# Batch 0 of attention: q cuts written and gathered before k, own turned rows for odd batches, first scores between two quarters of the next q and k

## What is computed

```python
qkv = hidden_states @ w_attn + b_attn
q, k, v = jnp.split(qkv, 3, axis=-1)             # 32 heads of 16 columns each
scores = jnp.einsum('bqhd,bkhd->bhqk', q, k) * SCALE
scores = jnp.where(causal[None, None], scores + bias[None], -jnp.inf)
attn = jax.nn.softmax(scores, axis=-1)
out = jnp.einsum('bhqk,bkhd->bqhd', attn, v).reshape(B, S, HIDDEN)
x = x + (out @ w_proj + b_proj)
```

## Time and profile before

| | |
|---|---|
| median of 3 runs | 704.13 us (703.55 to 704.23) |
| the profiled execution | 705.04 us |
| its span in the profile | 703.3 us |
| PE busy | 656.4 us, 93% |
| DVE busy | 478.5 us, 68% |
| ACT busy | 342.0 us, 49% |
| POOL busy | 92.0 us, 13% |
| mean granted clock of PE | 0.988 |

### The profile page before, as it was taken

One profiled execution on the slowest core, in us unless ns is written; L12 is line 12 of the kernel. 1 busy time (PEld: TensorE's weight loads), 2 busy tenths in 40 slices (PEclk: granted clock), 3 DMA queues, 4 the chain that ended last, 5 costly groups with the idle time before them and its releaser, 6 DMA issues.

```text
span 703.3 us, 10157 instructions
## 1 busy us (share of the span) xinstructions
PE 656.4 (93%) x3784; PEld 485.3 (69%) x3784; DVE 478.5 (68%) x906; ACT 342.0 (49%) x534; POOL 92.0 (13%) x189
## 2 busy tenths in 40 slices
PE   5988999999999886999999999999999999999997
PEld 4866688678676664887786665756756555787876
DVE  6755584894788779787693656365364797868565
ACT  5214554524534671442378996476482924435221
POOL 4411002102101042100141010100100220100000
PEclk9989999999999997999999999999999999999999
DMA  8494503505636040000062000000001305000000
GB/s 272 118 266 145 169 14 94 154 27 150 206 98 228 2 160 1 0 1 1 15 229 79 0 1 0 1 0 1 1 0 57 123 0 180 2 30 16 16 31 30
DMA packets 31763, 51.35 MB, mean 73 GB/s; under 512 B 3433, under 2 KB 17132, under 8 KB 30159
## 3 DMA queue, kind: packets, MB, share of 16 engines
q1 hardware_dynamic: 31138, 49.05, 21.8%
q10 hardware_dynamic: 576, 1.64, 1.0%
HBM read 42.09 MB, written 8.40 MB: 72 GB/s over the span
## 4 chain that ended last, share of the span: by engine, by line
PE 77%; DVE 13%; ACT 4%; issue 2%; DMA 1%; ACTq 1%; POOL 1%; SPq 0%; DVEq 0%; POOLq 0%
PE ps L1853 13%; PE ps L1820 12%; PE ps L2041 11%; PE ps L1980 10%; PE ps L1984 5%; PE ps L1683 5%; DVE nmax L1077 3%; PE ps L1761 2%; PE ps L1699 2%; PE ps L1829 2%; PE ps L1663 2%; PE ps L1751 2%; DVE prodT L1590 1%; DVE nmax L1074 1%; ACT sign_junk L966 1%
## 5 line engine op out<-in xcount | busy, mean ns | idle before, releaser
L2041 PE MATMUL ps<-wdT,prodT 128*128 128x512 f32 (+1 forms) x176 | 77.7, 597 | 0.4
L2041 PEld LDWEIGHTS ps<-wdT,prodT 128*128 128x128 f32 (+1 forms) x176 | 32.8, 190 | 40.7 <-issue 38.2
L800 ACT ACTIVATE probsT<-ps 128x1536 f32<-128x1536 f32 x32 | 46.1, 1450 | 28.9 <-PE ps L1751 28.7
L840 ACT ACTIVATE funs<-ps 128x512 f32<-128x512 f32 x16 | 9.5, 596 | 99.0 <-PE ps L1822 88.0
L669 POOL TENSOR_SCALAR ln_spread<-ln_moments 128x1 f32<-128x1 f32 x24 | 6.9, 287 | 299.4 <-DVE ln_moments L1148 299.4
L1154 DVE SCALAR_TENSOR_TENSOR junk<-x_sb,gate_row 128x512 f32<-128x512 f32 x48 | 43.1, 897 | 1.0
L1590 DVE COPY prodT<-ps 128x512 f32<-128x512 f32 (+1 forms) x24 | 13.7, 599 | 40.3 <-PE ps L2030 40.0
L1077 DVE TENSOR_REDUCE nmax<-ps 128x4 f32<-128x1024 f32 x32 | 38.9, 1215 | 0.0
L1417 DVE SCALAR_TENSOR_TENSOR x_sb<-b_row,coef,x_sb 128x512 f32<-128x512 f32 x48 | 37.0, 771 | 1.8
L966 ACT ACTIVATE sign_junk<-mlp_size_next,minus_guess 128x1376 bf16<-128x1376 f32 x24 | 34.6, 1443 | 0.8
L966 ACT ACTIVATE sign_junk<-mlp_size_main,minus_guess 128x1376 bf16<-128x1376 f32 x24 | 34.6, 1442 | 0.7
(11 more groups left out here) (282 smaller groups left out, 1725.0 us busy)
## 6 DMA issues: line engine op xcount, KB each, us to landing
cuts<-parts SPq DMA_DIRECT2D x16, 384.0 KB, 2.8
qst<-cuts SPq DMA_DIRECT2D x48, 128.0 KB, 2.6
w_first_raw<-in_L_ffn_w SPq DMA_DIRECT2D x6, 1024.0 KB, 7.7
w_second_raw<-in_L_ffn_w SPq DMA_DIRECT2D x6, 1024.0 KB, 9.0
kst<-cuts SPq DMA_DIRECT2D x36, 128.0 KB, 2.7
wqkv_raw<-in_L_attn_a_w_attn SPq DMA_DIRECT2D x3, 1024.0 KB, 8.2
wdT<-in_L_attn_b_w_down SPq DMA_DIRECT2D x1, 2560.0 KB, 10.1
wg_raw<-in_L_attn_b_w_gate SPq DMA_DIRECT2D x1, 2048.0 KB, 7.9
```

Source lines behind the costliest of these rows:

```text
L800: nc.scalar.activation(probsT[:, g % 2, :].rearrange("p (k n) -> p k n", k=3), slot[g % 2], ACT.Exp).then_inc(exp_ok.sem, 1)
L2041: last = nc.tensor.matmul(ps[:, Y_BANK, :], prodT[0:m, c, :], wdT[0:m, c, :], start=(c == 0), stop=(c == IC - 1))
```

## The change

The parts of it, with the diff below cut to its core:

1. SP writes q of half 0 as soon as its third part is there, ahead of the six small bias loads, then q of half 1, then gathers q of both halves, each after its own write. ACT writes k of both halves after its last `second_part`, then gathers k of half 0. SP gathers k of half 1 after q.
2. POOL does the cut of batch 0's first quarter ahead of `ln(1)`.
3. Odd batches have turned rows of their own (`odd_rowsT_hi`, `odd_rowsT_lo`), and batch 1 turns into PSUM banks 0 and 1. PE turns the rows of batch 1 in front of the values of batch 0; DVE copies them before the last quarter's rest and makes the low part between the two values.
4. PE makes quarter 0 of batch 1 after the values, and quarter 1 between score groups 1 and 2 of batch 0. DVE makes the rest of quarter 0 after the maxima of group 1 and that of quarter 1 after the maxima of group 3.

```diff
+        odd_rowsT_hi = sb("odd_rowsT_hi", [P, KC, S], F32R)
+        odd_rowsT_lo = sb("odd_rowsT_lo", [P, KC, S], F32R)
...
+        def write_side(eng, b, half, side):
+            need(eng, part3, b, place(b, 2 * half + side) + 1)
+            eng.dma_start(cuts[side, half].rearrange("m (g p) t -> p (m g) t", p=P),
+                          parts[:, side, half].rearrange("p m g t -> p (m g) t")).then_inc(cuts_out[half].sem, 16)
...
         def row_banks(b):
-            return first_rows if b == 0 else work
+            return first_rows if b <= 1 else work
...
+            write_side(sp, 0, 0, 0)
             sp.wait_ge(bias_out, 16)
             sp.wait_ge(bias_zero, 2)
...
-            write_cuts(0, 0)
-            write_cuts(0, 1)
-            gather(0, 0, (0,))
-            gather(0, 1, (0,))
+            write_side(sp, 0, 1, 0)
+            for half in range(2):
+                need(sp, cuts_out[half], 0, 16)
+                send_rows(sp, 0, half, 0)
+            need(sp, cuts_out[1], 0, 16 * 2)
+            send_rows(sp, 0, 1, 1)
...
             constants()
+            cut(0, (0,))
             ln(1)
-            cut(0)
+            cut(0, (1, 2, 3))
...
             second_part(0, 3)
+            for half in range(2):
+                need(act, cuts_out[half], 0, 16)
+                write_side(act, 0, half, 1)
             need(act, cuts_out[0], 0, 16 * 2)
             send_rows(act, 0, 0, 1)
-            need(act, cuts_out[1], 0, 16 * 2)
-            send_rows(act, 0, 1, 1)
...
             residue(0, 1)
+            for j in range(TB):
+                turned_rows_high(1, j)
             residue(0, 3)
             dve.wait_ge(bias_v_in, 16)
-            for j in range(TB):
-                value(0, j)
-            for j in range(TB):
-                turned_rows_high(1, j)
+            value(0, 0)
             for j in range(TB):
                 turned_rows_low(1, j)
-            residue(1, 0)
-            residue(1, 1)
+            value(0, 1)
...
+            def first(g):
+                if g == 1:
+                    residue(1, 0)
+                elif g == 3:
+                    residue(1, 1)
...
-                maxima(b, lambda g: steady(b, g) if b >= 1 else None)
+                maxima(b, first if b == 0 else lambda g: steady(b, g))
...
+            turn_rows(1)
             for j in range(TB):
                 value(0, j)
-            turn_rows(1)
-            for f in range(2):
-                turned_part(1, f)
+            turned_part(1, 0)
             pe.wait_ge(alibi_in, 32)
             pe.wait_ge(consts, 11)
             for g in range(NG):
+                if g == 2:
+                    turned_part(1, 1)
                 scores(0, g)
             turned_part(1, 2)
             maxima(0)
```

More of the change, by code:

```diff
@@ L281, in build @@
         wqkv_lo = sb("wqkv_lo", [P, 3, KC, D], F32R, wqkv_at)
-        qk_bias = sb("qk_bias", [P, 2, HT], F32)
-        at[0] = wqkv_at + 3 * 4 * KC * D + 4 * TB * 2 * D
+        odd_rowsT_hi = sb("odd_rowsT_hi", [P, KC, S], F32R)
+        odd_rowsT_lo = sb("odd_rowsT_lo", [P, KC, S], F32R)
         parts = sb("parts", [P, 2, 2, 3, HT // 2, S], BF16)
@@ L290, in build @@
         wproj_hi = sb("wproj_hi", [P, KC, D], F32R)
-        rowsT_hi = sb("rowsT_hi", [P, KC, S], F32R)
-        rowsT_lo = sb("rowsT_lo", [P, KC, S], F32R)
+        even_rowsT_hi = sb("even_rowsT_hi", [P, KC, S], F32R)
+        even_rowsT_lo = sb("even_rowsT_lo", [P, KC, S], F32R)
         qst = sb("qst", [P, H, S], BF16)
@@ L301, in build @@
         rden = sb("rden", [P, 2, TB * G], F32)
+        qk_bias = sb("qk_bias", [P, 2, HT], F32)
         maskS = sb("maskS", [P, P], BF16)
@@ L488, in place @@
             return turned_order(b).index(f)
+        rowsT_hi, rowsT_lo = (even_rowsT_hi, odd_rowsT_hi), (even_rowsT_lo, odd_rowsT_lo)
         def turn_bank(b, f):
             return ps[:, 2 + f, :] if b == 0 else work[f % 2]
+        def write_side(eng, b, half, side):
+            need(eng, part3, b, place(b, 2 * half + side) + 1)
+            eng.dma_start(cuts[side, half].rearrange("m (g p) t -> p (m g) t", p=P),
+                          parts[:, side, half].rearrange("p m g t -> p (m g) t")).then_inc(cuts_out[half].sem, 16)
         def send_rows(eng, b, half, side):
@@ L533, in _ @@
             sp.dma_start(bias_cuts.rearrange("i (p n) -> p i n", p=P), bias_parts[:, :, :]).then_inc(bias_out, 16)
[L534 to L539, removed]
             def write_cuts(b, half):
@@ L543, in write_cuts, with gather @@
                 for side in range(2):
[L544 to L549, removed]
+                    write_side(sp, b, half, side)
+            def gather(b, half):
                 need(sp, sT_ps, b - 1, (half + 1) * GHALF)
                 need(sp, cuts_out[half], b, 16 * 2)
-                for side in sides:
+                for side in range(2):
                     send_rows(sp, b, half, side)
@@ L567, in load_wide @@
                 sp.dma_start(end[:, :, :], w[:, :, IM:I]).then_inc(here, 16)
-            write_cuts(0, 0)
-            write_cuts(0, 1)
-            gather(0, 0, (0,))
-            gather(0, 1, (0,))
+            write_side(sp, 0, 0, 0)
+            sp.wait_ge(bias_out, 16)
+            sp.wait_ge(bias_zero, 2)
+            for i in range(3):
+                sp.dma_start(bias_proj[32 * i:32 * i + 1, :], bias_cuts[i:i + 1, 0:D]).then_inc(bias_rows, 16)
+                sp.dma_start(bias1[32 * i:32 * i + 1, :, :].rearrange("a e n -> a (e n)"),
+                             bias_cuts[i:i + 1, D:]).then_inc(bias_rows, 16)
+            write_side(sp, 0, 1, 0)
[4 more added lines that the diff above has]
+            send_rows(sp, 0, 1, 1)
             sp.dma_start(x_sb[:, 2 * TB:T, :], x_v[:, 2 * TB:T, :]).then_inc(x_rest, 16)
@@ L655, in ln, with cut @@
                 nc.gpsimd.tensor_tensor(rstd[:, :], spread[:, :], neg_half[:, :], ALU.pow).then_inc(rstd_ok.sem, 1)
-            def cut(b):
-                for k, f in enumerate(turned_order(b)):
+            def cut(b, steps=range(4)):
+                for k in steps:
+                    f = turned_order(b)[k]
                     side, pair = f % 2, f // 2
@@ L744, in turned_rows @@
                     need(act, hT_ps, b, j + 1)
-                    nc.scalar.copy(rowsT_hi[:, :, j * P:(j + 1) * P],
+                    nc.scalar.copy(rowsT_hi[b % 2][:, :, j * P:(j + 1) * P],
                                    row_banks(b)[j].rearrange("p (c t) -> p c t", c=KC)).then_inc(hT_ok.sem, 1)
@@ L1024, in turned_rows_high @@
                 need(dve, hT_ps, b, j + 1)
-                nc.vector.tensor_copy(rowsT_hi[:, :, j * P:(j + 1) * P],
+                nc.vector.tensor_copy(rowsT_hi[b % 2][:, :, j * P:(j + 1) * P],
                                       row_banks(b)[j].rearrange("p (c t) -> p c t", c=KC)).then_inc(hT_ok.sem, 1)
@@ L1030, in turned_rows_low @@
                 at_j = slice(j * P, (j + 1) * P)
-                nc.vector.tensor_tensor(rowsT_lo[:, :, at_j], row_banks(b)[j].rearrange("p (c t) -> p c t", c=KC),
-                                        rowsT_hi[:, :, at_j].bitcast(F32), ALU.subtract).then_inc(hT_low.sem, 1)
+                nc.vector.tensor_tensor(rowsT_lo[b % 2][:, :, at_j], row_banks(b)[j].rearrange("p (c t) -> p c t", c=KC),
+                                        rowsT_hi[b % 2][:, :, at_j].bitcast(F32), ALU.subtract).then_inc(hT_low.sem, 1)
             def turned_heads_low(b, j):
@@ L1639, in turn_rows @@
                 for j in range(TB):
-                    if b >= 1:
+                    if b == 1:
+                        need(pe, hT_low, 0, j + 1)
+                    elif b >= 2:
                         need(pe, v_out, b - 1, j + 1)
@@ L1662, in value @@
                     for c in range(KC):
-                        last = nc.tensor.matmul(work[j], rows[:, c, at_j], weight[:, 2, c, :],
+                        last = nc.tensor.matmul(work[j], rows[b % 2][:, c, at_j], weight[:, 2, c, :],
                                                 start=(i == 0 and c == 0), stop=(i == 2 and c == KC - 1))
@@ L1671, in turned_part @@
                     need(pe, res1, b, f - 1)
-                elif b >= 1:
+                elif b == 1:
+                    need(pe, v_out, 0, f + 1)
+                elif b >= 2:
                     need(pe, hT_low, b, f + 1)
@@ L1683, in turned_part @@
                             last = nc.tensor.matmul(turn_bank(b, f)[:, m * S:(m + 1) * S], weight[:, side, c, columns],
-                                                    rows[:, c, :], start=(i == 0 and c == 0),
+                                                    rows[b % 2][:, c, :], start=(i == 0 and c == 0),
                                                     stop=(i == 2 and c == KC - 1))
```

## The result

The kernel with the change took 709.74 us, the median of 6 runs (706.84 to 710.36), beside 704.44 for the kernel before in 6 runs: a ratio of 1.0062, with a 95% interval of 1.0043 to 1.0082. A second set of 6 runs beside 16 of before gave 707.92 and 703.9, ratio 1.0061 (1.0039 to 1.0083). The change makes the kernel slower by 0.6%, some 4.3 us. The ratio is not the quotient of the two medians, which lie 5.3 us apart in the first set and 4.0 in the second. The 12 executions of the kernel after spread widely: four took 706.1 to 706.9 us, one 708.4, and seven 709.2 to 710.4. The two that were traced are those of 708.40 and 706.14 us, so none of the seven long ones is seen from inside. The profiled execution took 708.4 us, 706.7 of it span. Busy times are as before, 655.1 us of PE and 477.6 of DVE, so it is waiting that was added.

What follows compares the result with a forecast made beforehand. It took DVE's maxima of batch 0, behind the gathers, as the bound. First scores at 41.0, two groups to 44.7, quarter 1 to 47.6, group 2 to 48.7, the rest to 60.2: +1.9 on 58.30, giving 706.0 us (702.5 to 709.0).

Steps and rivals of the forecast that it cites:

- the signs named: Before 65 us: sixth gather at 36 or later, scores near 41, PE idle over 4 us, DVE waiting before group 2.
- the upper bound: All costs up to the last maximum together: k at 42.8 and half clock through quarter 1 (+2.3), +6.8 us.
- Queue of ACT: ACT issues the k half 0 write at 29.1 and the sixth gather at 36.2; first scores at 41.0.
- the bounds 2.6 and 6.6: Shortest and longest landing time in us of k half 0's sixth gather, so it lands between 38.8 and 42.8.
- The count in bytes: Landing of k half 0: 4.0 MB ahead or beside at 238 to 285 GB/s take 14 to 17 us.
- From the first scores on: Batch 0's scores and maxima: half clock for two groups, quarter 1 between groups; last maximum at 60.2, +1.9 us.
- The base: Last maximum of batch 0 in the kernel before at 58.30, 16.4 us after the first scores, taken from its profile.
- The collision: POOL's first cut and DVE's weight rest, 19 to 30 us: DVE waits until 20.3, 0.45 us late.
- (a): Gathers of k half 0 land early at 38.8 and PE's clock holds: gain of 1.8 us, 702.3 us; chance 0.18.
- (b): Both halves cancel: first scores at 40, clock back early in quarter 1, +0.2 to +1.2, 704.8 us; chance 0.28.
- (c): ACT's k half 0 write starved by SP's q gathers: k some 3 us later, +4.9, 709.0 us; chance 0.12.

Runs made afterwards that it cites:

- e4: The kernel with the change, but SP gathers q half 1 only once k half 1 is written too, behind k half 0's write; 705.43 us, ratio 1.0021.
- e2: The kernel with the change, plus five repeats of the first 12 matmuls of batch 1's quarter 0 to keep PE busy; 707.55 us, ratio 1.0041.
- e6: The kernel with the change, but PE makes quarter 1 of batch 1 before the scores, DVE's rests staying between the maxima; 706.19 us, ratio 1.0034.
- e1: The kernel with the change, its part 4 undone: quarter 1 before all scores, both rests before the maxima; 705.59 us, ratio 1.0008.
- e3: The kernel before with part 1 of the change alone (the new queue order); 704.92 us, ratio 1.0009.
- e9: The kernel before with part 1 alone, in the form of e4 (k half 0 ahead of q half 1); 701.82 us, ratio 0.9958.
- e5: The kernel with the change, with the edits of e4 and e1 together; 700.92 us, ratio 0.9957.
- e7: The kernel with the change, unchanged, run again for more executions and a second trace; 707.92 us, ratio 1.0061.
- e10: The kernel before with part 3 alone (own turned rows for batch 1, turned before the values); 704.19 us, ratio 0.9990.

## Why the prediction was right, and where its size was off

**Direction and place.** Slower was forecast as likeliest and came. The median of 709.74 is 3.7 us above the 706.0 given, and 0.7 above the range of 702.5 to 709.0. Measured against the kernel before in the same set, the ratio of 1.0062 on the base of 704.13 gives 708.5, which is inside the range. The loss, some 4.3 us, is over twice the 1.9 forecast. The steps that carried the sign held: the last maximum of batch 0 sets the end, the gathers of k half 0 come hardly sooner in spite of the earlier q (the first scores 0.3 and 0.7 us earlier than before, 0.9 forecast), and what was moved between the score groups is paid there. Of the signs named, one failed (the sixth gather issued at 36 or later: it was 34.57); the idle PE, the clock of 0.5 behind it, the wait of DVE at group 2 and the unchanged length behind 65 us came. One sum was wrong in itself: with k at 42.8 (+1.8) and half clock through quarter 1 (+2.3) the upper bound is 1.9 + 1.8 + 2.3 = +6.0, and +6.8 only with group 2 at half clock as well.

**Queue of ACT: two errors that cancelled in part, by luck.** I had the k half 0 write issued at 29.1, behind the end of the last `second_part`. That copy ended at 28.23 instead of 29.1, and the write was issued at 27.67, when the copy had just started:

```profile
27.61 0.62 ACT L790 CAST parts<-resid 128x512 bf16<-128x512 f32 x1 [0.94 <-DVE resid L1076]
27.67 2.28 ACTq L498 DMA_DIRECT2D cuts<-parts  x2
31.39 3.79 ACTq L506 DMA_DIRECT2D kst<-cuts  x6
```

The sixth gather was thus issued at 34.57, not 36.2, but its landing took 6.85 us where I took 4.8 between the bounds 2.6 and 6.6. The bound was even a little short. First scores: forecast 41.0, measured 41.56 and 41.20, where the right issue time with my 4.8 us would have given 39.4. PE was done with quarter 0 at 34.1, 1.2 us before the forecast 35.3; this only made its idle time longer, 7.5 us instead of 5.7. The count in bytes, 40.2 to 43, was the better guide, and its reading, that q half 1 stands ahead of k half 0, is what e4 shows.

**From the first scores on: the term that was mis-sized.** My step said two groups at 1.86, quarter 1 in 2.9 and group 2 in 1.1, all later groups at full clock: 19.2 us between first scores and last maximum. The second trace has 19.0, the first 20.7. In the first, the last maximum is 62.23 - 60.2 = 2.0 us behind the forecast. Of this 0.6 is the later start, and 0.9 lies between there and the first maximum of group 2: groups 0 and 1 took 2.1 and 2.0 us, quarter 1 3.3 and group 2 1.3 (forecast 1.86, 1.86, 2.9 and 1.1). The last 0.5 is the clock, which fell again behind PE's waits at groups 4 to 6 and made DVE wait 0.56 us at groups 6 and 7. A second fall is nowhere in my sum. The second trace, with no second fall, ends at 60.19, on the forecast 60.2, and its execution was the shortest of the twelve. So the sum describes the short executions of the kernel, and even the first trace is 0.8 us shorter than the shortest of the seven long executions. What these lose beyond it stays open. e2 gives the clock's share as about a third of the loss; e6 and e1 give quarter 1 about half of it and the rests of DVE the other half, both with the clock's share in them. That most of the loss hangs on part 4 is shown by e1; these shares of it are rough. Nor is part 4 the only way to be rid of it: with part 4 in place, e4 takes back some two thirds by the order of the gathers alone.

**The base.** In the profiled execution of before, PE fell to half clock at 47 us, and DVE waited there; I took its 58.30 as the kernel's own. e3 and e9, on the same PE program, needed 15.3 us between first scores and last maximum, not 16.4. Of the 1.1 us between them, 0.4 is DVE's second rest, which in the kernel before ends behind the first scores, and 0.7 lies in the maxima themselves, where the clock fell. So some of what I booked as cost of the old order was chance of one execution, and the difference of the medians (5.3 and 4.0 us) was larger than that of the first traces (3.4). Whether a fall at 47 us is missing in most executions of before is not shown. Their mean clock (0.990 to 0.993 in 52 of 71, 0.988 in the profiled one) can't tell, since the profiled one also has the lower clock at another place: 0.74 in the window from 260 to 280 us, where the kernel after has 0.83.

**POOL and DVE.** The collision came as forecast: the cut took 1.17 us and the weight rest beside it 2.66 instead of 2.26, while POOL's tiny instruction behind that took 2.28:

```profile
18.86 1.17 POOL L672 TENSOR_TENSOR parts<-resid,parts 128x512 bf16<-128x512 f32 x1 [4.39 <-ACT parts L790]
19.99 2.28 POOL L662 TENSOR_SCALAR spread<-moments 128x2 f32<-128x2 f32 x1
```
```profile
19.52 2.66 DVE L1054 SCALAR_TENSOR_TENSOR wqkv_lo<-wqkv_raw,wqkv_hi 128x2048 fp32r<-128x2048 f32 x1
...
23.12 1.00 DVE L1032 TENSOR_SCALAR h_sb<-x_sb,moments,rstd 128x512 f32<-128x512 f32 x2 [0.16 <-POOL rstd L664]
```

The same small instruction took 0.23 us at 5.77 us in this trace, where nothing stood in its way. The one that issues first goes on undisturbed, as the Trainium skill, SBUF — State Buffer, Who interferes with whom, says; the trace agrees in both directions, with 0.4 us lost by DVE and 2.05 by POOL. What I had too large was the consequence: the norm of batch 1 was to be ready at 23.5, 0.5 late, and POOL finished its `rstd` at 23.08, 0.07 later than before, since DVE's weight rest had begun 0.3 us earlier. With no cut beside them the two normed tiles then took 1.00 us instead of 2.68. This is how the last `second_part` came to end at 28.23.

**The rivals.** (a) fell: k half 0 landed at 41.4, not 38.8, and the clock was lost. (b) fell too: the insertion was not hidden by DVE, which waited 1.60 and 1.00 us for it. (c) was nearest in its time and wrong in its mechanism. The k half 0 write took 3.71 us beside the q gathers against 2.82 before, 0.9 us more and not 3, and in e4, with fewer q gathers beside it, still 3.59. In the nine traces with the new queues whose chain shows this write it took 3.1 to 3.8 us, so it was not starved by the gathers of the other queue. That a DMA engine takes turns between queues a packet at a time (the Trainium skill, DMA: Bandwidth & Descriptors, Queues, rings and completion order) did not lead to that case here. What was slow was the gathers: the sixth of k half 0 landed 6.3 to 7.1 us after its issue with q half 1 ahead of it, and 4.0 to 4.4 us without (e4, e5, e9).

## What to carry to other kernels

When the DMA engines are full, work out in bytes what stands ahead of the transfer that is waited for, and put behind it all that is needed later: six gathers of 128 KB moved behind it were worth 2.5 us. Do not place an engine's own work between the steps of another engine's chain while the first of them can do it during a wait in front. And see whether the one execution that a sum starts from had a fall of the clock in the stretch: two executions of one kernel differed by 2.0 us here, where the whole loss was 4.3.

## What the runs showed of the hardware

- A DMA issue on ACT's queue did not wait for the end of the copy that stands in front of it in the program: the copy ran from 27.61 to 28.23 us, the issue was at 27.67. In e1, e3, e4 and e9 it also came 0.06 us behind the start of the copy (e3: 28.95 and 29.01). Here this was harmless, since the write needed only POOL's result.
- After the same wait of 1.38 us of PE the granted clock went to half in the kernel before and in e3, and stayed at full in e9. It stayed at full too after the waits of 1.62 us (e3) and 1.33 us (e9) for the gathers. After the waits of 2.4 to 7.5 us for the gathers (after, e7, e1, e4, e5, e6, e10) it fell each time, though not always at once: in e10, after 3.8 us, the window from 40 to 42 us still has 1.00 and the next one 0.73.
